# A second copy of a normalised activation, laid out by tile, as the stationary operand of a bias product

## The reference, cut to what matters

```python
def _L0_conv_ref(x, w1, b1, w2, b2, bias_w, bias_b):
    bias = x @ bias_w.T + bias_b                      # the bias product
    xf = jnp.fft.rfftn(xb, axes=(1, 2), norm='ortho')
    xr, xi = (xf.real, xf.imag)
    r1 = relu(_block_mul(xr, w1[0]) - _block_mul(xi, w1[1]) + b1[0])
    i1 = relu(_block_mul(xr, w1[1]) + _block_mul(xi, w1[0]) + b1[1])
    r2 = _block_mul(r1, w2[0]) - _block_mul(i1, w2[1]) + b2[0]
    i2 = _block_mul(r2, w2[1]) + _block_mul(i1, w2[0]) + b2[1]
    out = jnp.fft.irfftn(jax.lax.complex(r2, i2), s=(H, W), axes=(1, 2), norm='ortho')
    return out.reshape(B, H, W, C) + bias
x = x + _L0_conv_ref(_gn(x), ...)
```

## Time and profile before

| What | Value |
|---|---|
| Median of three runs | 428.96 us (428.8 to 429.08) |
| The profiled execution, its own time | 430.57 us |
| Its span, from the first to the last instruction | 428.7 us |
| PE busy, PEld busy | 397.9 us (93%), 351.2 us (82%) |
| DVE, ACT, POOL busy | 289.4, 228.8, 84.0 us |
| Mean granted TensorE clock | 0.983 |
| PE's share of the chain that ended last | 89% |

### The profile page before, as it was taken

The page is one execution under the profiler, slowest core; times in us unless marked ns, Lnnn a source line. Parts: engine busy times, 40 slices in busy tenths (PEclk is TensorE's granted clock), DMA queues, the critical chain, the costliest instruction groups (busy, mean ns, idle before and its releaser), DMA issues.

```text
span 428.7 us, 19333 instructions
## 1 busy us (share of the span) xinstructions
PE 397.9 (93%) x8578; PEld 351.2 (82%) x8578; DVE 289.4 (68%) x728; ACT 228.8 (53%) x514; POOL 84.0 (20%) x72
## 2 busy tenths in 40 slices
PE   4468799999999999998999999998999999998996
PEld 4367689788898889887897889887898988986894
DVE  4787677864787657774678657865578747877525
ACT  2884766256752666446662576436653567426420
POOL 0000001800054000900036000810018000691000
PEclk9859999999999999999999999999999999999999
DMA  6670000170004300170003600161001800040004
GB/s 217 193 242 2 2 3 5 57 276 3 5 15 167 157 3 4 40 294 4 3 4 125 211 3 5 41 247 49 3 5 39 297 3 3 19 170 3 5 3 149
DMA packets 12408, 32.98 MB, mean 77 GB/s; under 512 B 4963, under 2 KB 6661, under 8 KB 12325
## 3 DMA queue, kind: packets, MB, share of 16 engines
q1 hardware_dynamic: 12324, 31.74, 21.0%
HBM read 16.00 MB, written 12.58 MB: 67 GB/s over the span
## 4 chain that ended last, share of the span: by engine, by line
PE 89%; ACT 4%; issue 2%; DVE 2%; DMA 1%; DVEq 0%; SPq 0%; ACTq 0%
PE bank L574 89%; DMA x_sb<-in_x 1%; ACT y L914 1%; ACT junk L902 1%; ACT yraw L894 1%; ACT r L924 1%; ACT biasw L928 1%; DVE o_sb L1126 0%; ACT w2s L928 0%; DVE r L1110 0%; ACT z L934 0%; ACT junk L905 0%; DVE w1R L1031 0%; DVE rho L1031 0%; ACT rho L953 0%
## 5 line engine op out<-in xcount | busy, mean ns | idle before, releaser
L574 PE MATMUL bank<-biasw,y 128*64 128x384 f16 x1152 | 110.8, 336 | 0.0
L574 PEld LDWEIGHTS bank<-biasw,y 128*64 128x64 f16 x1152 | 93.5, 196 | 1.8 <-issue 0.3
L574 PE MATMUL bank<-w2s,rho 128*64 128x96 f16 x3072 | 85.2, 207 | 0.6 <-issue 0.6
L574 PEld LDWEIGHTS bank<-w2s,rho 128*64 128x64 f16 x3072 | 80.3, 109 | 4.6 <-issue 3.2
L879 POOL TENSOR_TENSOR x_sb<-x_sb,added 128x384 f32<-128x384 f32 x56 | 74.8, 1369 | 0.0
L574 PE MATMUL bank<-w1R,y 128*128 128x192 f16 (+3 forms) x768 | 60.4, 228 | 6.5 <-ACT y L914 3.4
L1031 DVE SCALAR_TENSOR_TENSOR rho<-bank,rho 128x256 f16<-128x256 f32 (+2 forms) x128 | 39.9, 364 | 33.7 <-ACT rho L953 24.1
L934 ACT ACTIVATE z<-bank 128x384 f16<-128x384 f32 x72 | 35.3, 490 | 50.5 <-PE bank L574 49.5
L877 POOL TENSOR_TENSOR x_sb<-x_sb,added 128x384 f32<-128x384 f32 x8 | 8.1, 1009 | 268.5 <-DVE yraw L1097 268.5
L919 ACT ACTIVATE g<-bank 128x384 f16<-128x384 f32 x64 | 30.2, 481 | 53.0 <-PE bank L574 53.0
L574 PE MATMUL bank<-tab,x_sb 128*128 128x128 f32 x384 | 51.2, 290 | 7.3 <-DMA x_sb<-in_x 5.8
(11 more groups left out here) (113 smaller groups left out, 413.9 us busy)
## 6 DMA issues: line engine op xcount, KB each, us to landing
x_sb<-in_x SPq DMA_DIRECT2D x16, 768.0 KB, 7.2
out<-o_sb SPq DMA_DIRECT2D x14, 768.0 KB, 3.9
y<-y SPq DMA_DIRECT2D x24, 128.0 KB, 2.7
out<-o_sb SPq DMA_DIRECT2D x8, 192.0 KB, 1.9
tab<-in_tab SPq DMA_DIRECT2D x1, 672.0 KB, 5.0
o_sb<-in_bias_wt SPq DMA_DIRECT2D x4, 144.0 KB, 2.7
b1raw<-in_b1h SPq DMA_DIRECT2D x1, 384.0 KB, 5.4
g<-in_w2t SPq DMA_DIRECT2D x2, 144.0 KB, 2.6
```

The source lines that it names most:

```text
L574: return nc.tensor.matmul(o, lhsT, rhs, start=start, stop=stop, **kw)
```

## The change

A new buffer `yt` holds a second copy of y, in which the 64 columns of each tile stand side by side. For the images 1 to 7 POOL fills it with six `tensor_copy` instructions of 1024 float16 columns each (two halves, three channel tiles), which read with a step of 16 bytes and write without gaps. They wait for the last `c2_rho` of the image before (`g_prod`), which is behind the last reader of the old `yt`. In POOL's program they stand ahead of the `add_map` of the same image. On PE the first bias product of each of these images waits for all six copies, and all eight bias products of the image read `yt`. Image 0 reads y as before.

```diff
@@ -237,6 +237,7 @@
         y = [sb(f"y{p}", [128, 2, KT, 2, 512], f16) for p in range(2)]
+        yt = sb("yt", [128, 2, NT, 2, 512], f16)
@@ -768,11 +770,14 @@
+                if gi == 0 and not first:
+                    pe.wait_ge(yt_ready, 2 * NT * b)
                 bank = g_bank(gi, more)
                 for ct in cts:
                     for of, w in ((0, 0), (0, 1), (1, 0)):
                         for part in range(2):
-                            mm(bank[64 * part:64 * part + 64, 0:CH], y[p][:, of, ct, part, gi:512:8], biasw[:, w, ct, :],
+                            columns = y[p][:, of, ct, part, gi:512:8] if first else yt[:, of, ct, part, 64 * gi:64 * gi + 64]
+                            mm(bank[64 * part:64 * part + 64, 0:CH], columns, biasw[:, w, ct, :],
@@ -878,9 +883,20 @@
+            def by_tile(b):
+
+                pool.wait_ge(g_prod, 8 * b)
+                for s in range(2):
+                    for ct in range(NT):
+                        pool.wait_ge((yh_ready, yl_ready)[s], NT * b + ct + 1)
+                        nc.gpsimd.tensor_copy(yt[:, s, ct, :, :].rearrange("k a (t m) -> k a t m", t=TILES),
+                                              y[b % 2][:, s, ct, :, :].rearrange("k a (m t) -> k a t m", t=TILES)).then_inc(yt_ready, 1)
+
             for b in range(BATCHES):
+                if b > 0:
+                    by_tile(b)
                 pool.wait_ge(dve_step, NSTEP * min(b + 2, BATCHES))
                 add_map(b)
```

More of the change, by code:

```diff
@@ L377, in spectral_block_kernel @@
         yl_ready = sem("yl_ready")
+        yt_ready = sem("yt_ready")
         z_prod, zh_ready, zl_ready = sem("z_prod"), sem("zh_ready"), sem("zl_ready")
```

## The result

The changed kernel took 425.42 us (median of 10 runs, 424.55 to 428.82) against 429.89 us for the kernel before, timed anew with it (10 runs, 428.8 to 432.0). The ratio is 0.9909, 95% interval 0.9889 to 0.9929: 0.91% faster. The forecast was 425.1 us, a ratio of 425.1 / 428.96 = 0.9910. The profiled execution has a span of 422.7 us and its own time is 424.55 us.

The account below looks back on a forecast made before the run. PE's stream was taken as the bound; six images at 552 ns (3.31 us) plus 536 ns in image 7 save 3.85 us, copies hidden: 428.96 - 3.85 = 425.1 us, range 424.1 to 428.1.

Parts of the forecast that it names:

- What bounds the kernel: PE's stream: busy 93% of the span; in bias products loads hide under 384-column matmuls, leaving only the first pair to gain.
- The loads: First pair of each bias product, images 1 to 7: 88 ns saved behind another array shape, 72 ns behind rho.
- The wait behind tile 1: PE's wait for rho ahead of step 5 of `p4` absorbs the 88 ns saved in tile 1's product.
- the saving ahead of step 4: Image 7, `p4`: a saving of 88 ns there brings a nearly vanished wait back, so nothing was counted.
- The copies: Six POOL copies at 2.0 us each, 12.0 us in all, fully hidden; chance 0.50.
- the lower bound: Price of a 1024-column POOL copy taken from the 288-column copy: 1.5 us.
- Rival 3: Bias product loads do not get shorter and the time stays at 429.0 us; chance 0.05.
- The windows: Time for POOL's six copies before the next first bias product: 19.6 us in images 1 to 6, 13.8 in image 7.
- the rivals: PE waits for copies: image 7 alone, 2.3 to 2.94 us a copy, chance 0.28; over 2.94 us, slower, chance 0.17.
- the break-even: Copy price at which PE's wait in image 7 eats the whole gain: 2.94 us a copy.
- The neighbours: DVE beside POOL's copies in c1 and `p3`: nothing added, z keeping its usual 556 ns.
- the stops: Four PE stops without shown cause, 3.6 us in all, at fixed program places; one coming or going worth about 1 us.

## Why the prediction was right

The mechanism held at each step of the sum. That the time came out within 0.3 us of the forecast is in part luck: the measured change itself is known to about 0.9 us either way.

*What bounds the kernel*: right. The stream of a product was bound by its moving columns, and of the 86 ns by which a load got shorter only the first pair's part counted.

*The loads*: 438 to 350 ns and 398 to 326, so 88 and 72 as taken. An image gained 0.57 us against 0.552.

*The wait behind tile 1*: right, and shown by the pair of kernels with tile 1 and tile 2 on the old operand: 47.98 and 48.08 us an image against 48.00. In image 7 too the saving ahead of step 4 came back as a wait, as the forecast had it: the piece from there to the bias product took 1.46 us before and takes 395.76 - 394.21 = 1.55 now.

*The copies*: 2.0 us each, as taken from between 1.5 and 3.6. The value was a choice between bounds far apart, given a chance of 0.50, and that it hit was luck. The bounds did not hold the price of every form: packed it is 1.0 us, below the lower bound; with a write in steps of 128 bytes it is 4.6, above the upper. The row of 288 columns behind the lower bound was itself not packed on the write side (three of every four elements), was float32, and had a guessed fixed part of 0.1 us; which of these made the bound too high is not shown. The Trainium skill's rule on stepped reads (GPSIMD Engine Reference, Performance pitfalls for Q7 kernels) would have given an estimate of 2.5 us; the direction agrees, with 2.0 us for a read in steps of 16 bytes against 1.0 packed, and the time is shorter here. Rival 3 is out: the loads do get shorter. The Trainium skill's TensorE: Matmul & The Clock Gate, section LDWEIGHTS, has a time by the number of columns alone, and the traces disagree: 64 columns take 196 ns with a step of 16 bytes and 110 packed.

*The windows*: right. In image 7 PE waited 4.15 us where six more microseconds of copies met 1.8 us of slack (6.0 - 1.8 = 4.2), and the copies with stepped writes made PE wait as long as both windows say, 14.1 us in image 7 and 8.4 in the images 2, 4 and 6. What a wait there costs was under-sized in the rivals: 1.28 us of half clock come on top, so the break-even is nearer than 2.94 us a copy; how short a wait already costs this was not tried.

*The neighbours*: z beside the copies stayed at 556 ns, and the copies unused cost nothing that the runs show.

*What the prediction left open*: the stops. It gave them 3.6 us in all and took them as fixed to their places. With them gone the time falls by 3.4 us, about as much as the change itself brings. They are not a matter of the place alone: they hang on the 1.5 MB load at the start of an image. What the store beside it adds was not tried by itself.

## What to carry to other kernels

A slow operand load costs only where no longer matmul covers it: count the first pairs of each group, not the busy time, and check for each saving that the next wait of that engine moves with it. Before moving a group of matmuls into a gap, ask which later chain it was covering. When an engine stops in the middle of a unit that has no wait there, at the same count of instructions each time, look at the large transfers in flight: late instructions of its own are a candidate, not shown here, and spreading the transfers was worth 0.7 to 0.8%.

## What the runs showed of the hardware

- 64 float16 stationary columns load in 110 ns packed or with a step of 4 bytes, in 193 to 196 ns with a step of 16 bytes.
- GpSimd copies 1024 float16 columns in 1.0 us packed, 2.0 us with reads in a step of 16 bytes, 4.6 us with packed reads and writes in a step of 128 bytes, and 2.1 us (as two halves) with reads in a step of 16 bytes and writes in a step of 4.
- In a wait of PE of 4.15 us the granted clock fell to 0.50 while PE still stood; over the next 2.9 us it was 0.54, and 18 matmuls took 2.86 us instead of 1.58.
